# Score products of an attention layer on 32-row groups of the array, with compact keys

## What is computed

```python
x = x + 0.5 * ffn(layernorm(x))       # 16 experts, top 4, and a shared one
x = x + attn(layernorm(x))
x = x + 0.5 * ffn(layernorm(x))

# attn: 32 query heads of 8, 8 key/value heads, causal
q, k, v = x @ Wq + bq, x @ Wk + bk, x @ Wv + bv
q, k = rope(q), rope(k)
scores = einsum('bhqd,bhkd->bhqk', q, repeat(k, 4)) / sqrt(8)
scores = where(kpos > qpos, -inf, scores)
out = einsum('bhqk,bhkd->bhqd', softmax(scores), repeat(v, 4)) @ Wo + bo
```

## Time and profile before

| | |
|---|---|
| median of 3 runs | 843.28 us (841.11 to 844.68) |
| span of the profiled execution | 841.5 us |
| TensorE busy | 740.7 us, 88% |
| VectorE busy | 460.5 us, 55% |
| ScalarE busy | 373.8 us, 44% |
| GpSimd busy | 188.6 us, 22% |
| attention | about 280 to 577 us |

### The profile page before, as it was taken

How to read it: one execution, slowest core, us unless ns; L and a number is a source line. 1 busy time by engine, 2 the same in 40 slices (tenths; PEclk the granted TensorE clock), 3 DMA queues, 4 the chain that set the end, 5 groups by cost and what they waited for, 6 DMA issues and landing times.

```text
span 841.5 us, 13291 instructions
## 1 busy us (share of the span) xinstructions
PE 740.7 (88%) x4776; PEld 393.5 (47%) x4776; DVE 460.5 (55%) x942; ACT 373.8 (44%) x569; POOL 188.6 (22%) x158
## 2 busy tenths in 40 slices
PE   4547999999998588999999999996645999999998
PEld 2224656566565333333343444543323565665655
DVE  6314554555456987799978887645313333333334
ACT  6213334344343747646666676776202232222322
POOL 1017333433434513000000000001013333333332
PEclk9877999999998679999999999997967999999999
DMA  5794444434430000000000000000694222122122
GB/s 167 40 29 138 137 122 114 123 113 122 120 89 26 1 1 1 1 1 1 1 2 1 1 2 1 1 2 1 19 28 90 69 75 75 50 75 75 55 70 76
DMA packets 16169, 44.37 MB, mean 53 GB/s; under 512 B 2658, under 2 KB 5090, under 8 KB 16132
## 3 DMA queue, kind: packets, MB, share of 16 engines
q1 hardware_dynamic: 12388, 33.65, 21.2%
q10 hardware_dynamic: 3744, 10.23, 4.0%
HBM read 40.58 MB, written 1.19 MB: 50 GB/s over the span
## 4 chain that ended last, share of the span: by engine, by line
PE 78%; DMA 8%; DVE 6%; ACT 4%; SPq 2%; issue 1%; POOL 1%; DVEq 0%; ACTq 0%; POOLq 0%
PE psum L861 49%; PE psum L1025 8%; DMA R<-oT 8%; PE psum L1009 7%; PE psum L998 7%; PE psum L996 2%; SPq L361 2%; PE psum L1012 2%; DVE m_part L811 2%; PE psum L983 1%; ACT kT L567 1%; ACT xT L474 1%; PE psum L1032 1%; DMA x_res<-x_dram 1%; DVE kaug L801 0%
## 5 line engine op out<-in xcount | busy, mean ns | idle before, releaser
L861 PE MATMUL psum<-xT,W_hi 128*128 128x512 f16 x880 | 266.3, 385 | 0.0
L383 POOL TENSOR_TENSOR R<-R 128x512 f32<-128x512 f32 x112 | 151.4, 1354 | 346.2 <-DVE R L722 237.5
L861 PE MATMUL psum<-W_hi,R 128*128 (+1 forms) x896 | 168.9, 278 | 53.9 <-DVE R L722 53.9
L811 DVE TENSOR_REDUCE m_part<-psum 128x1 f32<-128x512 f32 (+3 forms) x384 | 188.2, 551 | 42.3 <-PE psum L998 40.0
L708 DVE SCALAR_TENSOR_TENSOR R<-psum,R 128x512 f32<-128x512 f32 x108 | 74.6, 691 | 209.5 <-ACT R L495 209.5
L495 ACT ACTIVATE R<-psum 128x512 f32<-128x512 f32 x108 | 64.3, 596 | 246.9 <-PE psum L861 246.9
L582 ACT ACTIVATE R<-psum 128x1024 f32<-128x1024 f32 x144 | 141.8, 1024 | 68.1 <-PE psum L1009 45.7
L861 PE MATMUL psum<-xT,W_lo 128*128 128x512 f16 x440 | 168.5, 383 | 0.0
L861 PEld LDWEIGHTS psum<-xT,W_hi 128*128 (+1 forms) x880 | 87.1, 99 | 83.9 <-issue 4.2
L861 PEld LDWEIGHTS psum<-W_hi,R 128*128 128x128 f16 x896 | 89.1, 99 | 78.6 <-issue 37.2
L861 PE MATMUL psum<-W_lo,R 128*128 (+1 forms) x448 | 124.5, 278 | 0.0
(11 more groups left out here) (101 smaller groups left out, 456.4 us busy)
## 6 DMA issues: line engine op xcount, KB each, us to landing
R<-coef_dram SPq DMA_DIRECT2D x60, 256.0 KB, 3.9
w_stage<-w_dram ACTq DMA_DIRECT2D x26, 384.0 KB, 3.0
R<-coef_dram SPq DMA_DIRECT2D x8, 448.0 KB, 3.5
R<-coef_dram SPq DMA_DIRECT2D x8, 384.0 KB, 3.4
R<-coef_dram SPq DMA_DIRECT2D x6, 320.0 KB, 3.5
R<-coef_dram SPq DMA_DIRECT2D x6, 192.0 KB, 3.8
x_res<-x_dram SPq DMA_DIRECT2D x8, 128.0 KB, 2.2
R<-oT SPq DMA_DIRECT2D x4, 256.0 KB, 16.7
```

The lines of the kernel that those rows point to most:

```text
L383: nc.gpsimd.tensor_tensor(hc[:, c, :], v[:, j, c, :], C[:, j, c * CH:(c + 1) * CH], ALU.mult).then_inc(s_hc[c], 1)
L811: nc.vector.tensor_reduce(m_part[:, h, kc:kc + 1], ps[:, 0:n], axis=AX.X, op=ALU.max).then_inc(free_of(e), 1)
L861: ins = nc.tensor.matmul(o, stat(a, k), mov(b, k), start=first and n == 0, stop=last and n == 3 * k_parts - 1, **kw)
```

## The change

The score products contract over the 32 partitions of their own head group. `kT` holds two slabs of 1024 columns in place of eight, one for each group of four key heads, with every partition in use. Both operands of L998 and L1009 are cut to 32 partitions. The copy of `kx` is one instruction, the memset of `kT` and its wait go, and `qkvo_f` has memory of its own. In `st` the two score products stand next to each other and the masks follow. Four costs of the planner's table change, and with them the order of the events.

```diff
         if kind == "kx":
-            return [(PE, 0.15), (ACTE, 1.1)], [("sp", t)]
+            return [(PE, 0.15), (ACTE, 0.4)], [("sp", t)]
...
-            return [(PE, 0.06 + cols / 2400), (DVE, 0.07 + cols / 960)], [("q1", e[2])]
+            return [(PE, 0.06 + cols / 7200), (DVE, 0.07 + cols / 960)], [("q1", e[2])]
...
-            return [(PE, 0.9 if diag else 0.45), (ACTE, 0.95)], [("q2", e[3]), ("st", e[1] - 1, e[2])]
+            return [(PE, 0.7 if diag else 0.25), (ACTE, 0.95)], [("q2", e[3]), ("st", e[1] - 1, e[2])]
...
-        kT = sb("kT", [P, NKV, T], F16)
-        qkvo_f = kT[:, :, :].rearrange("p g n -> p (g n)").bitcast(F32)[:, 0:KC * (QKV + D)]\
-            .rearrange("p (k n) -> p k n", k=KC)
+        kT = sb("kT", [P, GHI, T], F16)
+        qkvo_f = sb("qkvo_f", [P, KC, QKV + D], F32)[:, :, :]
...
             def constants():
-                pool.wait_ge(s_qkvo_l, 1)
-                nc.gpsimd.memset(kT[:, :, :].rearrange("p g n -> p (g n)").bitcast(F32), 0.0)
...
-                    for g in range(GLO):
-                        rows = slice(ROW * g, ROW * (g + 1))
-                        ins = nc.scalar.activation(kT[rows, g:NKV:GLO, t * P:(t + 1) * P], ps[rows], ACT.Copy)
-                    ins.then_inc(free_of(e), 1)
+                    nc.scalar.activation(kT[:, :, t * P:(t + 1) * P], ps, ACT.Copy).then_inc(free_of(e), 1)
...
-                    g = h // (GQ * GLO) * GLO + h % GLO
+                    gh, rows = h // (GQ * GLO), slice(ROW * (h % GLO), ROW * (h % GLO + 1))
...
-                    nc.tensor.matmul(out_bank[:, 0:n], qT1[:, i % 2, h // GLO, :],
-                                     kT[:, g, kc * 512:kc * 512 + n], start=not diag, stop=True,
+                    nc.tensor.matmul(out_bank[:, 0:n], qT1[rows, i % 2, h // GLO, :],
+                                     kT[rows, gh, kc * 512:kc * 512 + n], start=not diag, stop=True,
...
                     for gl in (2 * pair, 2 * pair + 1):
-                        ins = nc.tensor.matmul(bank[gl], kT[:, gh * GLO + gl, kt * P:(kt + 1) * P],
-                                               qT2[:, u % 4, :, :], start=True, stop=kt != t)
+                        rows = slice(ROW * gl, ROW * (gl + 1))
+                        ins = nc.tensor.matmul(bank[gl], kT[rows, gh, kt * P:(kt + 1) * P],
+                                               qT2[rows, u % 4, :, :], start=True, stop=kt != t)
+                    for gl in (2 * pair, 2 * pair + 1):
                         if kt == t:
```

## The result

The changed kernel takes 925.6 us (median of four: 919.1, 920.5, 930.7, 950.7) against 843.0; the ratio is 1.096, with a 95% interval of 1.092 to 1.100. The forecast was 838.1 us, with a range of 813 to 868. Executions with products on 32 rows scatter more than those of the kernel before, and their time goes with TensorE's mean granted clock over the span: 919.1 us at 0.857, 930.7 at 0.839, 950.7 at 0.820 (before: 841 to 847 us at 0.940 to 0.947).

What follows compares the result with a forecast made beforehand. The prediction took TensorE's stream of columns as the bound, VectorE close behind. Its terms, -31.1 - 19.9 + 48.3 - 3 - 1 + 1.5 = -5.2 us, took 843.3 to 838.1 us, range 813 to 868.

Steps and rivals of the forecast that it cites:

- step 6: End of attention's event list: the last maximum's chain stands directly before the last score products, +1.5 us (bounds 0 and +3).
- step 3: Units ahead of the fifth of 16: idle TensorE time covers most of the added shape changes there, -3 us.
- signs named for steps 1 and 2: L1009 pairs starting within 0.02 us; mask to L998 product 0.15 us; 512-column L998 to next mask 0.31 us.
- Step 1: Attention's score products: neighbours in different row groups run together, -31.1 us inside `st` events and -19.9 us elsewhere.
- further overlaps: Neighbouring row-group score products beyond the pairs inside `st` events: worth at most 22.9 us, taken at 19.9.
- Step 2: TensorE's list in attention: 514 more changes of product shape at 0.094 us each, +48.3 us.
- Steps 4 and 5: ScalarE's copy into kT becomes one instruction, -1 us; kT's memset in the first feed-forward part goes, zero.
- five rivals: Forecast holds 0.45; free row-group changes 0.18; switches eat the gain 0.20; dearer changes 0.11; row groups don't overlap 0.06.

Runs made afterwards that it cites:

- nomask128: The kernel before without both mask products, all score products over 128 rows: 835.1 us.
- st32: The kernel before with only the transposed score products (L1009) on 32 rows, from a compact copy of the keys, order unchanged: 844.4 us, ratio 1.002.
- oldorder: The changed kernel with the planner's four costs set back, so the event list is that of the kernel before: 878.8 us.
- colmask: The kernel before with each small mask product cut into four of 32 stationary columns, score products still over 128 rows: 884.8 us.
- neworder128: The kernel before, all products on 128 rows, with only the planner's four new costs: 874.5 us, ratio 1.038.
- ffn32: The kernel before with the second feed-forward part's products on 32 rows only and TensorE's loop there written out: 1035.1 us.

## Why the prediction was wrong

Three steps failed: the clock, a term put at nothing without a reason; step 6, the order, taken at 1.5 us where it costs 32; and step 3, the cover, 3 us the wrong way. The signs named for steps 1 and 2 came true, and yet the time is 58 us above the top of the range.

**The bound.** Right in kind: TensorE sets the pace, VectorE close behind. The slip is that no engine stands alone: nomask128 takes 28 us off TensorE's streams for 7 us of time, and st32 gets none of its 7.

**Step 1, overlap.** Right: row groups run together. Of the further overlaps as much as 7 us may be missing in oldorder's second part alone, against 3 allowed for in the whole list.

**Step 2, changes of shape.** Right: 0.10 us where 0.094 was taken, in both directions, and 420 of them cost 42 us in colmask. The rule of the Trainium skill in "TensorEngine Tiling (Array Packing)" (Key Properties), that changing the mode drains TensorE, is borne out for row groups by this 0.10 us. The reason given for the choice of 0.094 was wrong, though: the results of the new products start at partition 0 and fill all 128; it is their operands that start at others. So the price was met with some luck. In oldorder's second part, at full clock, what steps 1 and 2 are about comes to +7 us.

**Step 3, cover.** Wrong in its sign. The early, loosely filled units were to hide 3 us. In oldorder they are where the clock fell, from 0.96 to 0.75, and they take 27 us more. The sign named for this step, VectorE's busy time from 302 to 360 us as before, isn't there: 39.7 us in oldorder and 34.4 in the changed kernel against 44.5.

**Steps 4 and 5.** As priced, and too small to be measured by themselves: one L562 of 384 ns per tile, and attention's stretch starts at the same time (294 us against 295).

```profile
L562 ACT ACTIVATE kT<-psum x8: 364/384/384, 284.3 to 333.2; 128x256 f16<-128x256 f16 x8
```

**Step 6, order.** The right mechanism with a wrong size: +1.5 us taken for the last maximum alone, +32 measured (neworder128). I priced the one place where the list visibly differed, at its end, and not that all four engines follow a list made for a TensorE two to three times as fast.

**What was not in the sum.** Every duration was read at 2.4 GHz and carried over, as if the clock were given. None of the five rivals had a changed clock in it. It was there to be asked: in the earlier trace rows the clock is 0.94 in the stretch where TensorE is filled least, 302 to 360 us, and 1.00 where it is full. How much it costs here can only be bounded: at a mean clock of 0.857 over 917 us TensorE ran at 1.2 GHz for 2 x 0.143 x 917 = 262 us, before for 2 x 0.057 x 841 = 96 us; 166 us more at half rate cost at most 83 us. The bound is above the whole loss of 76 us, so it excludes nothing. The experiments divide it better: list alone 32 us with the clock up (0.94), products alone 35 (7 of it with the clock up), and 9 to 21 that only both together lose.

That this last part is the clock's is argued. In the profiled execution the clock of the second part is 0.66, against 1.00 in oldorder and 0.99 in neworder128, but that is the longest execution. For those at 0.857 I estimate 0.75 over attention: 0.857 x 917 less 0.925 x 570 for the feed-forward parts (0.93 and 0.92 in the profile), over the 347 us left. Oldorder has 0.87 there and neworder128 0.96 (means of their two stretches above). Two stretches, of the changed kernel and of oldorder, show that the clock can be low with no wait at all in it:

```profile
539.00:593.00 54.00, 53.72 (x236) 11.31 (x238) 27.24 (x62) 24.75 (x27) 0.00 (x0) 0.50 0.00 1
```

```profile
575.00:600.00 25.00, 24.59 (x183) 9.84 (x178) 11.68 (x41) 16.66 (x21) 0.00 (x0) 1.00 0.01 2
```

Both have TensorE full with the same kinds of products, one at half rate and one at full. So a low clock isn't explained by the waits of its own stretch, and no run takes it apart further.

## What to carry to other kernels

Ask of every change that makes TensorE's work smaller or narrower what it does to the granted clock, above all where it isn't the only bound: the same products may then run at half rate. A product on 32 rows can only pay where several of them stand next to each other, with no full-array product between, since each change of shape costs 0.1 us, half a 512-column product; no run here shows it to pay. And if a planner lays out in-order queues from a table of costs, a cost that is too small on the bounding engine is itself a regression: change the costs alone, on the old kernel, to see its price.

## What the runs showed of the hardware that I had not expected

A dense stream of products over 32 of 128 rows, busy 308.4 of 310 us, is granted 0.50 of the clock throughout; on 128 rows the control stream gets 1.00 (ffn32). Two row-group products start within 0.01 us of each other (oldorder, at 480.17), and a change into or out of their shape costs 0.10 us. The page "TensorE: Matmul & The Clock Gate" of the Trainium skill (Part 1) ties the clock to how busy TensorE has been; here it was busy 99% of the time, and the clock went with the number of rows.
